# Row sums ahead of the turned splits, the eighth unit of the first output tile taken later, and GpSimd's gathers and row stores in another order

## The reference

```python
x = L0_attn_x                                    # (4, 1024, 256)
x = _layernorm(x + attention(x), axis=-1)        # 16 heads, softplus magnitudes, angles
x = _layernorm(x + _L0_ffn_ref(x, ...), axis=-1) # mixture of experts

# _L0_ffn_ref: N = 4096 tokens, E = 8 experts, capacity 640 rows each
gates = softmax(x_flat @ router_w + router_b)
_, topk_idx = top_k(gates, 2)                    # each token goes to two experts
# every expert takes its first 640 tokens into buf
h = gelu(einsum('ecd,edh->ech', buf, w1) + b1[:, None, :])   # 256 -> 1024
out = einsum('ech,ehd->ecd', h, w2) + b2[:, None, :]         # 1024 -> 256
y = sum over experts of out[token's row] * gate
```

## Time and profile before

| | us |
|---|---|
| median of three runs | 974.79 (972.11 to 976.84) |
| the profiled execution | 970.69 |
| its span | 968.9 |
| TensorE matmul busy | 911.5 (94%) |
| ScalarE busy | 728.8 (75%) |
| VectorE busy | 602.7 (62%) |
| GpSimd busy | 455.0 (47%) |
| from the first turn of an expert to that of the next, experts 1 to 2 | 31.9 |

### The profile page before, as it was taken

One profiled execution on the slowest core, in us unless ns is written; L12 is line 12 of the kernel. 1 busy time (PEld: TensorE's weight loads), 2 busy tenths in 40 slices (PEclk: granted clock), 3 DMA queues, 4 the chain that ended last, 5 costly groups with the idle time before them and its releaser, 6 DMA issues. The chain is left out here.

```text
span 968.9 us, 19742 instructions
## 1 busy us (share of the span) xinstructions
PE 911.5 (94%) x7569; PEld 513.2 (53%) x7569; DVE 602.7 (62%) x1162; ACT 728.8 (75%) x889; POOL 455.0 (47%) x382
## 2 busy tenths in 40 slices
PE   8799999999989999998999999998599999999995
PEld 6333343344333334333433433344599999989994
DVE  5666446547785555787555767347457676667675
ACT  6588878887777888787789789985265678567863
POOL 0265225144355634546464435423525455654574
PEclk9899999999999999999999999999799999999998
DMA  7759442333534335344342327231365434543311
GB/s 219 233 202 353 142 166 70 122 142 132 189 133 159 117 120 186 137 161 136 139 158 100 135 97 239 98 102 35 99 231 164 137 112 135 181 135 108 124 60 61
DMA packets 62201, 139.75 MB, mean 144 GB/s; under 512 B 10242, under 2 KB 31299, under 8 KB 61584
## 3 DMA queue, kind: packets, MB, share of 16 engines
q1 hardware_dynamic: 41040, 74.46, 24.0%
q0 software_dynamic: 21056, 63.93, 18.5%
HBM read 71.43 MB, written 66.54 MB: 142 GB/s over the span
## 5 line engine op out<-in xcount | busy, mean ns | idle before, releaser
L689 ACT ACTIVATE prob<-spsum 128x1024 f32<-128x1024 f32 x512 | 493.1, 1021 | 111.3 <-PE spsum L881 103.3
L905 PE MATMUL opsum<-prob,val 128*17 128x512 f32 x2048 | 271.3, 599 | 1.3 <-DVE oraw L1271 0.4
L881 PE MATMUL spsum<-area_q 32*128 32x512 f32 x1536 | 133.5, 429 | 5.7 <-DMA area_q<-aT 3.3
L881 PE MATMUL spsum<-stacks 32*128 32x512 f32 x1536 | 134.4, 425 | 1.6 <-ACT prob L689 1.0
L881 PEld LDWEIGHTS spsum<-area_q 32*128 32x128 f32 x1536 | 73.1, 185 | 118.5 <-ACT prob L689 63.6
L881 PEld LDWEIGHTS spsum<-stacks 32*128 32x128 f32 x1536 | 73.5, 183 | 115.5 <-ACT prob L689 63.5
L1279 DVE RECIPROCAL oden<-oden 128x256 f32<-128x256 f32 x62 | 108.7, 1753 | 2.1
L574 POOL TENSOR_TENSOR onorm<-oraw,oden 128x512 f32<-128x512 f32 x31 | 41.6, 1343 | 119.5 <-DVE oden L1279 115.1
L519 POOL TENSOR_TENSOR area_s<-emb,area_s 128x1024 fp32r<-128x1024 f32 x28 | 66.5, 2377 | 53.0 <-DVE area_s L1097 53.0
L517 POOL TENSOR_TENSOR square<-raw 128x512 bf16<-128x512 f32 x28 | 53.7, 1918 | 80.3 <-DVE raw L1077 80.2
L905 PEld LDWEIGHTS opsum<-prob,val 128*17 128x17 f32 x2048 | 36.1, 95 | 102.2 <-ACT prob L689 63.9
(11 more groups left out here) (212 smaller groups left out, 1227.1 us busy)
## 6 DMA issues: line engine op xcount, KB each, us to landing
split_scratch<-area_s POOLq DMA_DIRECT2D x60, 512.0 KB, 5.0
area_k<-in_w SPq DMA_DIRECT2D x16, 1024.0 KB, 7.4
stacks<-split_scratch SPq DMA_DIRECT2D x28, 512.0 KB, 5.5
area_q<-split_scratch SPq DMA_DIRECT2D x28, 512.0 KB
dispatched<-blank POOLq DMA_DIRECT2D x1, 5300.0 KB, 25.3
rows<-dispatched SPq DMA_DIRECT2D x7, 662.5 KB
res<-in_x SPq DMA_DIRECT2D x4, 1024.0 KB, 9.3
aT<-onorm SPq DMA_DIRECT2D x124, 32.0 KB
```

What stands on the lines that cost most here:

```text
L689: act.activation(prob[u % NPB][:], spsum[u % NSB][:].rearrange("p a n -> p (a n)"), ACT.Exp, scale=HD ** -0.5).then_inc(s_exp, 1)
L881: ins = pe.matmul(spsum[u % NSB][:, j % 2, :], kst[par][rows, a, P * kt:P * (kt + 1)], qst[par][rows, b, cols], start=i == 0, stop=i == 2 ...
L905: ins = pe.matmul(opsum[32 * j:32 * j + HD + 1, :], val[b % 2][:, kt, h0 + j, :], prob[(2 * s + j // 2) % NPB][:, HALF * (j % 2):HALF * (j ...
```

## The change

It moves work within the lists of four engines and changes which semaphore values GpSimd waits for. No computation is added or removed. TensorE: seven units of output tile 0, then the turn of tile 1, four units of output tile 1, the eighth unit of tile 0, and the rest of tile 1. VectorE: the row sum stands ahead of the split for t = 0 and 1, and behind it for t = 2 to 4; the weights' remainders come last. ScalarE: `normalise` in four lots at t = 0, 1, 3 and 4, `second_half` at t = 2. GpSimd: gather t waits for one unit more; the row stores of expert e - 1's tiles 0, 1, 2 come behind the sum stores of tiles 1, 2, 3, that of tile 3 behind unit 1 of the next first layer.

```diff
@@ -1397,8 +1397,6 @@
         block = ctx.enter_context(nc.Block())
 
 
-        TURNS = ((0,), (1,), (2,), (3,), (4,))
-
         @block.sync
         def _(sp):
             def load_rows(e):
@@ -1459,14 +1457,14 @@
                 if e:
                     store_sums(e - 1, ST - 1)
                 if e >= 2:
-                    store_outputs(e - 2, 2)
+                    pool.wait_ge(s_h, HK * e + 2)
                     store_outputs(e - 2, 3)
                 pool.wait_ge(s_index, e + 1)
                 if e:
                     pool.wait_ge(s_sum, 16 * ST * e)
                     pool.wait_ge(s_z, ST * e)
                 for t in range(ST):
-                    pool.wait_ge(s_h, HK * e + 2 + t)
+                    pool.wait_ge(s_h, HK * e + 3 + t)
                     gather_sums(e, t)
                 if e >= 2:
                     pool.wait_ge(s_h, HK * (e + 1))
@@ -1474,9 +1472,9 @@
                 for t in range(ST - 1):
                     if e < LAST:
                         store_sums(e, t)
-                    if e and t >= 2:
-                        store_outputs(e - 1, t - 2)
-            for t in range(2, ST):
+                    if e and t:
+                        store_outputs(e - 1, t - 1)
+            for t in range(ST - 2, ST):
                 store_outputs(LAST - 1, t)
             for t in range(ST):
                 store_outputs(LAST, t)
@@ -1498,6 +1496,21 @@
                                        rows[e % 2][:, t, P * k:P * (k + 1)], ident[:])
                 ins.then_inc(s_turn, 1)
 
+            def outputs(e, t, first, end):
+
+                n = ST * e + t
+                if first == 0 and n >= 2:
+                    pe.wait_ge(s_z, n - 1)
+                for m in range(first, end):
+                    if t == 0:
+                        pe.wait_ge(s_hid, HK * e + m + 1)
+                    for i, (a, b) in enumerate(TERMS):
+                        ins = pe.matmul(yp[n % 2][:, 0:DIM], hids[:, a, m, P * t:P * (t + 1)],
+                                        w2s[e % 2][:, b, m, :], start=m == 0 and i == 0,
+                                        stop=m == HK - 1 and i == 2)
+                if end == HK:
+                    ins.then_inc(s_y, 1)
+
             idle_products(pe, yp[1][:, 0:P], ident, 8)
             for t in range(ST):
                 turn(0, t)
@@ -1524,20 +1537,16 @@
 
                     pe.wait_ge(s_w2lo, KC * e)
                 for t in range(ST):
-                    if e + 1 < EXPERTS:
-                        for tt in TURNS[t]:
-                            turn(e + 1, tt)
-                    n = ST * e + t
-                    if n >= 2:
-                        pe.wait_ge(s_z, n - 1)
-                    for m in range(HK):
-                        if t == 0:
-                            pe.wait_ge(s_hid, HK * e + m + 1)
-                        for i, (a, b) in enumerate(TERMS):
-                            ins = pe.matmul(yp[n % 2][:, 0:DIM], hids[:, a, m, P * t:P * (t + 1)],
-                                            w2s[e % 2][:, b, m, :], start=m == 0 and i == 0,
-                                            stop=m == HK - 1 and i == 2)
-                    ins.then_inc(s_y, 1)
+                    if e + 1 < EXPERTS and t != 1:
+                        turn(e + 1, t)
+                    if t == 0:
+                        outputs(e, 0, 0, HK - 1)
+                        if e + 1 < EXPERTS:
+                            turn(e + 1, 1)
+                        outputs(e, 1, 0, HK // 2)
+                        outputs(e, 0, HK - 1, HK)
+                    else:
+                        outputs(e, t, HK // 2 if t == 1 else 0, HK)
 
         @block.scalar
         def _(act):
@@ -1606,10 +1615,10 @@
                 for t in range(ST):
                     if e + 1 < EXPERTS:
                         turned_high(e + 1, t)
-                        if t == 1:
+                        if e:
+                            normalise(e - 1, e - 1, ((0,), (1, 2), (), (3,), (4,))[t])
+                        if t == 2:
                             second_half(e + 1)
-                        if e and t >= 2:
-                            normalise(e - 1, e - 1, ((0, 1), (2, 3), (4,))[t - 2])
                     elif t == 0:
                         normalise(e - 1, e - 1, range(ST))
                 if e and e + 1 < EXPERTS:
@@ -1727,17 +1736,19 @@
                 if e:
                     tell_variances(e - 1, e - 1, slice(0, ST))
                 for t in range(ST):
-                    if e + 1 < EXPERTS:
-                        for tt in TURNS[t]:
-                            turned(e + 1, tt)
-                        if t:
-                            remainder(e + 1, t - 1)
+                    if e + 1 < EXPERTS and t >= 2:
+                        turned(e + 1, t)
                     prepare(e, t)
                     if e and t == 0:
                         scale_and_shift(e - 1, e - 1, slice(0, ST))
                     if e == LAST and t:
                         scale_and_shift(LAST + t - 1, e, slice(t - 1, t))
                     add_own(e, t)
+                    if e + 1 < EXPERTS:
+                        if t < 2:
+                            turned(e + 1, t)
+                        if t:
+                            remainder(e + 1, t - 1)
                     if e == LAST:
                         variance(e, t)
                         tell_variances(LAST + t, e, slice(t, t + 1))
```

## The result

| | before | changed | ratio, 95% interval |
|---|---|---|---|
| median | 974.38 us (6 runs) | 966.81 us (6 runs) | 0.9926 (0.9901 to 0.9951) |
| the profiled execution | 970.69 | 970.5 | |
| first turn (702.59, 709.47) to the end of the span | 266.3 | 259.0 | |

The forecast was 966.2 us, in a range of 962 to 971.5. The two profiled executions are about equally long because the changed one reached the first turn of the expert stage 6.9 us later, in code that the change does not touch; so I compare the stretch from that turn to the span's end. It is 7.3 us shorter.

A forecast was written before the change was run, and what follows sets the result against it. TensorE was taken as held by tile 0's late row sum, 1.29 us in each of six experts. Gain 9.2 - 0.65 = 8.6 us; from the median, 974.8 - 8.6 = 966.2 us, range 962 to 971.5.

The forecast's parts named there:

- The gap: TensorE's idle 1.29 us ahead of tile 2's products, experts 1 to 6; T0 is the start of tile 0's turn.
- the 1.54 forecast in general: Tile 2's products in experts 1 to 6 were to start 1.54 us sooner, 789.46 for 791.00 in expert 2.
- The wait for `hid`: TensorE's 0.16 us wait in expert 2 for the last hidden remainder: to vanish, giving next to nothing of its own.
- neither the gathers nor the last row store [...] should move against T0: GpSimd's queue: no shift against the start of tile 0's turn, 0, at most 0.5 us either way per expert.
- some 15 us to spare: SyncE's weight loads follow the weight remainders with some 15 us to spare, so nothing queued there is late.
- rival A: The row stores' landing bounds every expert from 2 on; 968.8 to 971.3 us, middle 970; chance 22%.
- the sign that was to show the forecast wrong: In most experts, VectorE idle ahead of tile 0's row sum, released by the output rows' landing.
- the 9.2 us forecast for the second layers: Gain in experts 1 to 6 before any landing loss: 6 x 1.54 = 9.2 us.
- a sum of 8.9: Total gain in us if expert 6's row store lands 0.3 earlier, by the skill's fixed 2.0 us; the trace's 2.3 was preferred.
- The term of 0.65 us for the landing: Gain lost where tile 0's row sum waits for the earlier output rows to land; taken for one expert of six.
- Rival C: Slower: row stores and gathers slow first-layer units by 0.49 us each, 993 us if all 56; chance 5%.
- The last expert: Expert 7: row sum of tile 0 still held by the landing, gain 0; 1.3 us the most the end can gain.

The follow-up runs named there:

- before_again: The kernel before, unchanged, run once more for a second profile; ratio 1.0010 to the kernel before, stretch from first turn to span's end 263.3 us.
- load_early: The changed kernel with the last weight remainder back ahead of tile 4's row sum, so the w2 load is issued earlier; ratio 0.9872 to the kernel before.
- load_late: The kernel before with only the last weight remainder moved behind tile 4's row sum, so the w2 load is issued later; ratio 0.9995.
- after_again: The changed kernel, unaltered, run once more for a second profile; ratio 0.9920 to the kernel before, stretch from first turn to span's end 257.5 us.
- queues_only: The kernel before with only GpSimd's and ScalarE's new orders from the diff; ratio 1.0040 to the kernel before.

## Why the prediction was right

**The gap closes as worked out.** Row sum ahead of the split, split started by ScalarE's copy, turn by the split, products 0.17 behind it: expert 1, which has no landing to wait for, went from 8.64 to 6.69, 1.95 against the 1.54 forecast in general; with even first layers it is 7.98 to 6.45, 1.53. Tile 0 takes its products at T0 + 4.8, and the row sum follows at 4.9 where nothing holds it, as said. The wait for `hid` is gone, but it is also gone in before_again, where the first layers are even; no gain from it is shown.

**The step that failed** is that "neither the gathers nor the last row store [...] should move against T0". I had looked at what GpSimd waits for by the index and the unit and taken the sums' landing as early, and I had given SyncE's weight loads "some 15 us to spare" without asking what they collide with. The load moved from 2.5 us ahead of the last sum store to 0.5 us behind it, and the landing of those sums, 6.6 us in expert 2 and as late as the load's own, now holds the gathers. load_early shows it from one side and load_late from the other. So rival A came true in most experts, and with it the sign that was to show the forecast wrong, VectorE idle ahead of tile 0's `eo`; but not by the route that A named. The landing of the row store itself took 2.1 to 3.3 us from its issue, less than the 3.3 to 3.8 used, but the issue was 1.3 to 2.7 us later. Of the 9.2 us forecast for the second layers the profile shows 1.95 + 0.97 + 1.07 + 1.53 + 1.05 - 0.56 = 6.0, less 1.4 in the tile at the lower clock; between the two even executions (before_again, after_again) it is 1.53 + 0.36 + 1.54 + 0.74 + 1.53 - 0.47 = 5.2.

The prediction also set an estimated landing 0.3 us earlier, and a sum of 8.9, against its own. The Trainium skill (DMA: Bandwidth & Descriptors, Anatomy of one DMA) adds to the fixed 2.0 us a term for the bytes, which that estimate left out; for 128 rows of 1 KB it is an estimated 0.3 us, so both come to the 2.3 us that the prediction read from the trace.

**The term of 0.65 us for the landing** was thus too small: between the even executions it is 9.2 - 5.2 = 4.0. That the total still came near the forecast (7.6 us between the medians, 8.6 forecast) is partly luck. In the first pair of profiles the second layers gave 6.0 - 1.4 us, and 2.2 more came from the first layers of the kernel before (100.8 against 98.6), which the forecast did not have and which no run shows to be an effect of the change. The ratio's interval, 4.8 to 9.6 us, spans the 5.8 of the even pair as well as the 7.3 of the first. Rival C did not occur in either profile of the changed kernel; its sign, first layers of over 15 us, is there in queues_only, and what makes them slow stays open. The last expert gained 0.3 to 0.4 us, as forecast near nothing.

## What to carry to other kernels

A DMA load that a buffer's last reader releases moves with that reader: when an engine's list is reordered, look at which transfer is issued just ahead of the load and who waits for it to land. A landing that is hidden behind another wait becomes the bound when that wait is removed; move its issue in the same change (here one line moved gave 4.8 to 6.4 us of the stretch). Compare the stretch that a change touches in more than one profile of each kernel: here 2 to 3 us of unevenness came and went.

## What the runs showed of the hardware

A small indirect store lands late beside a large load. With the 1 MB weight load issued 0.5 us behind it, the last sum store landed in 6.2 to 7.4 us, within 0.2 us of the load; with no weight load beside it, in 2.8 (after_again).

GpSimd's gathers fall into step with the first layer's units. In after_again, expert 6, five in a row start 1.74 to 1.93 us apart, near a unit's 1.76, where gathers not held run 1.33 to 1.36 apart (expert 5, 865.44 to 868.13):

```profile
895.32 1.63 POOL L1435 DMA_INDIRECT others<-sum_scratch,add_idx  x1 [3.55 <-PE hp L1531]
897.25 1.43 POOL L1435 DMA_INDIRECT others<-sum_scratch,add_idx  x1 [0.30 <-PE hp L1531]
898.99 1.44 POOL L1435 DMA_INDIRECT others<-sum_scratch,add_idx  x1 [0.30 <-PE hp L1531]
...
904.25 1.02 POOL L1452 DMA_INDIRECT out<-eo,add_idx  x1 [0.30 <-issue]
...
866.80 1.03 POOL L1435 DMA_INDIRECT others<-sum_scratch,add_idx  x1 [0.31 <-issue]
868.13 1.03 POOL L1435 DMA_INDIRECT others<-sum_scratch,add_idx  x1 [0.30 <-issue]
```

So the last row store behind the gathers went at T0 + 2.1 or T0 + 3.9, one unit apart, in 48 of 55 cases over the profiles that keep it there, and only twice between: in after_again first gathers 8.6 and 8.7 us behind the layer's start gave the former, 9.0 to 9.8 the latter. A few tenths in a landing thus cost 0.8 to 2.1 us of TensorE. The Trainium skill (SBUF — State Buffer, Who interferes with whom) lets a VectorE instruction with two SBUF inputs shut out a GpSimd instruction that reads SBUF; VectorE has one such remainder (0.83 us) in each unit, and the trace agrees with it: each of these five gathers ends 0.9 us behind the end of a remainder (897.78 and 898.68 for the second). But no run took that remainder away.

An idle stretch of 2.0 us of TensorE was followed by a granted clock of 0.63 over 4.65 us in the changed kernel (expert 6); one of 2.07 us in after_again was not: the clock stayed at 1.00, and its tile 2 (908.84) took 3.07 us.
